# Tables' products at later steps of the routing, and gate products in quarters of TensorE's array

## The reference, cut to what matters

```python
scores = jnp.einsum('ntd,ed->nte', x, gate_w)            # 8 experts
probs = jax.nn.softmax(scores, axis=-1)
g, m = jax.lax.top_k(probs.transpose(0, 2, 1), k)        # k = 2 * 1024 / 8 = 256 tokens
xin = x[batch_idx, m]
h = gelu(jnp.einsum('nekd,edf->nekf', xin, w1))
h = jnp.einsum('nekf,efd->nekd', h, w2)
out = zeros.at[batch_idx, m].add(g[..., None] * h)
```

## Time and profile before

| | |
|---|---|
| median of 3 runs | 2249.83 us (2249.73 to 2259.84) |
| profiled execution | 2256.85 us, its span 2255.1 us |
| mean granted clock of PE over the span | 0.982 |
| PE busy | 2170.4 us, 96% |
| DVE, POOL, ACT busy | 1462.7, 1366.0, 1003.1 us |

### The profile page before, as it was taken

One profiled execution on the slowest core, in us unless ns is written; L12 is line 12 of the kernel. 1 busy time (PEld: TensorE's weight loads), 2 busy tenths in 40 slices (PEclk: granted clock), 3 DMA queues, 4 the chain that ended last, 5 costly groups with the idle time before them and its releaser, 6 DMA issues.

```text
span 2255.1 us, 34185 instructions
## 1 busy us (share of the span) xinstructions
PE 2170.4 (96%) x12186; PEld 1617.8 (72%) x12186; DVE 1462.7 (65%) x3348; ACT 1003.1 (44%) x1903; POOL 1366.0 (61%) x1237
## 2 busy tenths in 40 slices
PE   6998998999999999999999999999999999999997
PEld 4455888888886666666657766567666588899997
DVE  5355687676757666556775577874877645976653
ACT  3421443444445455335554354542554425444443
POOL 2322666677537766556775476664676845767774
PEclk9899999999999999999999999999999999999999
DMA  4332644555441122213212222212220244545552
GB/s 131 133 134 64 175 108 108 118 135 151 118 116 42 53 57 76 66 39 85 74 37 80 66 66 67 57 50 64 75 76 20 76 133 111 131 113 145 126 150 29
DMA packets 145049, 206.06 MB, mean 91 GB/s; under 512 B 19432, under 2 KB 112112, under 8 KB 144880
## 3 DMA queue, kind: packets, MB, share of 16 engines
q1 hardware_dynamic: 120304, 170.30, 25.4%
q0 software_dynamic: 24576, 33.57, 8.8%
HBM read 130.03 MB, written 39.85 MB: 75 GB/s over the span
## 4 chain that ended last, share of the span: by engine, by line
PE 75%; DVE 7%; POOL 3%; issue 3%; ACT 2%; DMA 1%; SPq 1%; another core or an unknown queue 0%; POOLq 0%; DVEq 0%; ACTq 0%
PE psum L1299 12%; PE psum L1278 12%; PE psum L1425 11%; PE psum L1327 7%; PE psum L1390 7%; PE psum L1406 6%; PE psum L1450 5%; PE psum L1341 4%; PE psum L1355 3%; PE psum L1435 3%; POOL t_acc L2362 2%; DVE f_hlo L2106 1%; PE psum L1368 1%; DVE f_hhi L2104 1%; PE psum L1246 1%
## 5 line engine op out<-in xcount | busy, mean ns | idle before, releaser
L1687 ACT ACTIVATE t_p<-psum 128x512 f32<-128x512 f32 (+3 forms) x768 | 323.6, 492 | 293.8 <-PE psum L1406 284.4
L2362 POOL TENSOR_TENSOR t_acc<-t_acc,t_p 128x1024 f32<-128x1024 f32 (+3 forms) x256 | 417.5, 1631 | 14.5 <-ACT t_p L1687 0.5
L2281 POOL TENSOR_TENSOR f_wlo<-f_wst,f_whi 128x256 fp32r<-128x256 f32 x256 | 219.9, 920 | 172.7 <-ACT f_whi L1620 172.7
L1299 PE MATMUL psum<-f_whi,f_hhi 128*128 128x256 f32 x1024 | 296.0, 289 | 6.2 <-DVE f_hlo L2106 6.2
L1425 PE MATMUL psum<-t_p,t_v 128*64 128x512 f32 (+3 forms) x1536 | 288.8, 496 | 6.2 <-POOL t_p L2342 6.2
L1299 PE MATMUL psum<-f_whi,f_hlo 128*128 128x256 f32 x1024 | 291.4, 285 | 0.0
L1299 PE MATMUL psum<-f_wlo,f_hhi 128*128 128x256 f32 x1024 | 291.1, 284 | 0.0
L2104 DVE CAST f_hhi<-f_h 128x512 fp32r<-128x512 f32 x256 | 135.0, 527 | 223.3 <-ACT f_h L1638 172.1
L1638 ACT ACTIVATE f_h<-psum 128x512 f32<-128x512 f32 x256 | 153.1, 599 | 280.9 <-PE psum L1278 235.9
L1390 PE MATMUL psum<-t_qa,t_ka 128*128 128x512 f32 (+3 forms) x768 | 223.1, 370 | 1.9 <-DVE t_kb L2136 0.7
L2362 POOL TENSOR_TENSOR t_acc<-t_p 128x768 f32<-128x768 f32 x64 | 134.5, 2102 | 135.4 <-PE psum L1435 132.1
(11 more groups left out here) (284 smaller groups left out, 4439.3 us busy)
## 6 DMA issues: line engine op xcount, KB each, us to landing
f_wst<-in_L_ffn_w SPq DMA_DIRECT2D x64, 1024.0 KB
t_ka<-t_ka SPq DMA_DIRECT2D x64, 256.0 KB, 3.5
t_qb<-t_qa SPq DMA_DIRECT2D x64, 256.0 KB, 3.7
t_wk<-wkT SPq DMA_DIRECT2D x32, 256.0 KB, 4.0
t_wq<-wqT SPq DMA_DIRECT2D x32, 256.0 KB, 4.0
t_wv<-wvT SPq DMA_DIRECT2D x16, 512.0 KB, 5.1
normal<-f_xy SPq DMA_DIRECT2D x5, 1024.0 KB, 10.2
a_x<-in_L_attn_a_x SPq DMA_DIRECT2D x4, 1024.0 KB, 10.1
```

Source lines behind the costliest of these rows:

```text
L1299: m = pe.matmul(out, h[:, js], w[:, f, :], start=(f == 0 and a == 0 and j % 2 == 0), stop=(f == FT - 1 and a == 2), skip_group_check=True)
L1687: act.activation(p[:, i, q0:], k.bank[bank][:, q0:], ACT.Exp, scale=1.0 / float(np.sqrt(k.DH))).then_inc(k.drained[bank], 1)
L2281: m = pool.tensor_tensor(t["wlo"][n % 2][:, i, ks], t["wst"][:, i, ks], t["whi"][n % 2][:, i, ks].bitcast(F32), ALU.subtract)
L2362: pool.tensor_tensor(acc[:, :, q0:], (p0 if kt == 1 else acc)[:, :, q0:], p[:, :, q0:], ALU.add).then_inc(k.p_acc, 1)
```

## The change

1. **Steps of the tables.** Thresholds get one step more before `threshold_rows` in routes 0, 1 and 3. The first sequence's table is no longer called behind its own column, but behind the second sequence's `hot_places` (in route 0 after four more empty steps). The second table comes after four (route 0) or two empty steps, together with the first `table_move`; the second `table_move` follows one (route 0) or three steps later. In route 0 the first table moves from step 39 to 44, the second from 43 to 49, of 56 steps.
2. **Gate products of routes 1 and 3.** `gateT` is widened with zeros to 32 columns per half of the channels. It is now the weights: 8 matmuls, each into 32 partitions of a bank (one quarter of the array's columns) with 256 tokens of `yT` passing. Scores then stand with experts on partitions. Two steps later `gate_turn` follows: ACT copies the bank's 128x256 into `wide`, and PE transposes it in two 128x128 blocks into the score bank, where `softmax_max` reads it with a stride of 32. So each sequence's scores take two more steps.
3. `pe_gate` goes; ACT's `row_transpose` waits for the bank of the gate product instead. A filling tile grows by 48 to keep addresses apart.

```diff
-        t["gate"], t["gateT"] = sb("f_gate", [E, D]), sb("f_gateT", [P, self.DT, E])
+        t["gate"], t["gateT"] = sb("f_gate", [E, D]), sb("f_gateT", [P, self.DT, 32])
...
+    def gated(self, t, i):
+        return t["wide"][:].rearrange("p n b e j -> p (n b e j)")[:, 2 * i * P:2 * (i + 1) * P]
...
         self.thresholds(r, t)
-        for _ in range(4 if r % 2 else 2):
+        for _ in range(5 if r % 2 else 3):
             yield
...
-        apart = [None] * 2 if r else []
+        steps = lambda first, later: [None] * (later if r else first)
         for i in range(2):
             self.hot_digits(r, i, t)
-            yield from apart
+            yield from steps(0, 2)
             self.hot_places(r, i, t)
-            yield
-            yield from apart
+            yield from steps(1, 2)
+            if i:
+                yield from steps(4, 0)
+                self.table(r, 0, t)
+                yield
             self.column(r, i, 0, t)
-            yield from apart
+            yield from steps(0, 2)
             self.column(r, i, 1, t)
-            yield
-            yield from apart
-            if i:
-                self.table_move(r, 0, pair[0], t)
-                yield
-            self.table(r, i, t)
-            yield
+            yield from steps(0, 2)
+        yield from steps(4, 2)
+        self.table_move(r, 0, pair[0], t)
+        self.table(r, 1, t)
+        yield from steps(1, 3)
         self.table_move(r, 1, pair[1], t)
         yield
...
             self.gate_product(r, i, t)
             yield
+            yield
+            self.gate_turn(r, i, t)
+            yield
...
     def gate_product(self, r, i, t):
...
-        for n in range(k.NBLK):
-            for dt in range(k.DT):
-                m = pe.matmul(sc[:, i, n, :], t["yT"][:, dt, n * P:(n + 1) * P], t["gateT"][:, dt, :],
-                              start=(dt == 0), stop=(dt == k.DT - 1))
-        m.then_inc(k.filled[b] if i else k.pe_gate, 1)
+        b = self.take(("gated", r, i), self.others[0])
+        for dt in range(k.DT):
+            rows = t["yT"][:, dt, :].rearrange("p (h g l) -> p h g l", h=2, l=P)
+            for g in range(4):
+                m = pe.matmul(k.bank[b][32 * g:32 * (g + 1), 0:2 * P], t["gateT"][:, dt, :], rows[:, :, g, :],
+                              start=(dt == 0), stop=(dt == k.DT - 1), skip_group_check=True)
+        m.then_inc(k.filled[b], 1)
...
+    def gate_turn(self, r, i, t):
+        k, pe = self.k, self.e
+        b, _ = k.where["score", r]
+        self.wait_drained(("gated", r, i))
+        for h in range(2):
+            m = pe.transpose(k.bank[b][:, (2 * i + h) * P:(2 * i + h + 1) * P], k.gated(t, i)[:, h * P:(h + 1) * P],
+                             k.ident[:])
+        if i:
+            m.then_inc(k.filled[b], 1)
...
+    def gate_turn(self, r, i, t):
+        k, act = self.k, self.e
+        b = self.wait_filled(("gated", r, i))
+        act.copy(k.gated(t, i), k.bank[b][:, 0:2 * P]).then_inc(k.drained[b], 1)
...
+        dve.memset(t["gateT"][:, :, k.E:], 0.0).then_inc(k.d_const, 1)
+        dve.tensor_copy(t["gateT"][:, :, 0:k.E], k.bank[b][:, 0:k.DT * k.E].rearrange(
             "p (k e) -> p k e", e=k.E)).then_inc(k.drained[b], 1)
...
+            row = 32 if r else k.E
+            sc = k.bank[b][:, 0:2 * k.NBLK * row].rearrange("p (n x) -> p n x", x=row)[:, :, 0:k.E]
```

More of the change, by code:

```diff
@@ L114, in semaphores @@
         self.d_scd = s("dve_early_scores")
-        self.pe_gate, self.a_probs = s("pe_gate"), s("act_probs")
+        self.a_probs = s("act_probs")
         self.a_split, self.d_split, self.p_split = s("act_whi"), s("dve_wlo"), s("pool_wlo")
@@ L271, in attention_tiles @@
         self.early_counts(st, early)
-        sb("t_room", [P, 64])
+        sb("t_room", [P, 112])
         heads(1)
@@ L412 @@
     mixed_norm = mixed_rows = mixed_transpose = mixed_gate = mixed_store = skip
-    route_load = route_store = row_transpose = gate_product = softmax_max = softmax_sum = prob_transpose = skip
+    route_load = route_store = row_transpose = gate_turn = gate_product = softmax_max = softmax_sum = prob_transpose = skip
     row_turn = row_scores = half_wide = count = digits = thresholds = threshold_rows = compare = rank = positions = skip
@@ L1147, in mixed_gate @@
             for dt in range(k.DT):
-                m = pe.matmul(sc[:, s, i, :], yT[:, s, dt, :], t["gateT"][:, dt, :], start=(dt == 0),
+                m = pe.matmul(sc[:, s, i, :], yT[:, s, dt, :], t["gateT"][:, dt, 0:k.E], start=(dt == 0),
                               stop=(dt == k.DT - 1), skip_group_check=True)
@@ L1170, in gate_product @@
         k, pe = self.k, self.e
-        b, _ = k.where["score", r]
-        sc = k.bank[b][:, 0:2 * k.NBLK * k.E].rearrange("p (b n e) -> p b n e", b=2, e=k.E)
         self.wait_drained(("gate", 0))
+        self.wait_ge(k.d_const, 8)
         for c in range(2):
@@ L1199, in row_scores @@
             for dt in range(k.DT):
-                m = pe.matmul(k.bank[bank][:, i * k.E:(i + 1) * k.E], t["yT"][:, i, dt, :], k.f[0]["gateT"][:, dt, :],
+                m = pe.matmul(k.bank[bank][:, i * k.E:(i + 1) * k.E], t["yT"][:, i, dt, :], k.f[0]["gateT"][:, dt, 0:k.E],
                               start=(dt == 0), stop=(dt == k.DT - 1))
@@ L1574, in row_transpose @@
         if i:
-            self.wait_ge(k.pe_gate, (r + 1) // 2)
+            self.wait_filled(("gated", r, 0))
         elif r == 1:
@@ L1788, in gate_transpose @@
         b = self.wait_filled(("gate", layer))
-        dve.tensor_copy(t["gateT"][:], k.bank[b][:, 0:k.DT * k.E].rearrange(
+        dve.memset(t["gateT"][:, :, k.E:], 0.0).then_inc(k.d_const, 1)
+        dve.tensor_copy(t["gateT"][:, :, 0:k.E], k.bank[b][:, 0:k.DT * k.E].rearrange(
             "p (k e) -> p k e", e=k.E)).then_inc(k.drained[b], 1)
@@ L1898, in softmax_max @@
             b = self.wait_filled(("score", r))
-            sc = k.bank[b][:, 0:2 * k.NBLK * k.E].rearrange("p (b n e) -> p (b n) e", b=2, e=k.E)
+            row = 32 if r else k.E
+            sc = k.bank[b][:, 0:2 * k.NBLK * row].rearrange("p (n x) -> p n x", x=row)[:, :, 0:k.E]
             taken = k.drained[b]
```

## The result

The changed kernel takes 2244.34 us (median of 9 runs, 2236.72 to 2245.88), the kernel before, now with nine runs as well, 2258.01 (2249.73 to 2263.76). The ratio is 0.9948, 95% interval 0.9930 to 0.9966: 8 to 16 us less, 11.7 at its middle. The forecast of 15.4 us is a ratio of 0.9932 and lies inside the interval, near its end; the forecast time of 2234.4 us is 9.9 us too low.

A forecast was written before the change was run, and what follows sets the result against it. PE (TensorE) bounds the kernel, busy 2170.4 of 2255.1 us. Terms 9.4 - 2.1 - 3.9 + 6.8 + 4.9 - 0.3 + 0.6 + 1.0 - 1.0 = 15.4 us off 2249.83 give 2234.4 us; range 2225 to 2247.

The forecast's parts named there:

- The time: Whole kernel: 15.4 us less than 2249.83, the median of the profiled execution's neighbours, giving 2234.4 us.
- Gate product: Four gate products, routes 1 and 3: quarters side by side take 1.05 us plus 0.1 for tiling changes; 9.4 us saved.
- Turns' transposes: After each gate product: two new PE transposes, taken as 4 records, 0.52 us each turn; 2.1 us lost in all.
- Turn waits: PE waits for ACT's gelu, then copy, at three of four turns, 1.3 us each; 3.9 us lost.
- a turn that waits over 2 us: At the gates' turns: listed as a sign that the prediction is wrong; waits of 1.3 us were expected.
- Clock: Behind the four gate products: none of the four half-clock falls remains, 1.7 us each; 6.8 us gained.
- Tables: Route 1's first table: its 3.30 us wait and the half clock behind it go, 4.9 us gained; route 3's tables 0.
- Ranks: Route 1's compare comes behind U3, so PE waits before rank: 1.3 us lost, net -0.3 with thresholds' 1.0 gain.
- Route 0's end: End of stage A: second table ends 1.9 us earlier, moving the gather, less half of 1.7; net 1.0 us gained.
- rival 5: More than forecast: the stall at 328 us dissolves too (3.7 us), ACT and DVE lose nothing; 2228 us, chance 0.05.
- Attention: The attention part between stage 0 and stage 1: forecast change 0 us.

The follow-up runs named there:

- a2: The changed kernel again, unchanged, on a second chip: 2240.86 us, 0.9941 of the kernel before.
- e3: Kernel before, with each gate product's 32 records cut into 12, 12 and 8 at three following steps: 2250.59 us, 1.0017 of the kernel before.
- e5: Changed kernel with 16 extra records of the quarters' shape, all into one quarter, ahead of each gate product: one run, 2260.52 us.
- a3: The changed kernel again, unchanged, on a third chip: 2244.30 us, 0.9949 of the kernel before.
- e2: Kernel before with only the gate products in quarters and their turns, all other steps as before: 2241.07 us, 0.9967 of the kernel before.
- e1: Kernel before with only the new steps of thresholds and tables, gate products as before: 2253.51 us, 1.0023 of the kernel before.
- e9: e1 with route 3's rank left at its old step: 2253.70 us, 0.9993 of the kernel before.

## Why the prediction was right and wrong

*The time: the step that failed.* 8.2 of the 9.9 us are the base, not the sum: I applied 15.4 us to 2249.83, a median of three, as it stood 0.3% below the profiled execution. With nine runs before's median is 2258.01. In the trace a step of this size shows near the program's start: PE stands at half clock there for 30.7 us in eight of the fourteen profiles and for 13.7 in four (17.1 and 27.3 in the other two), and the part up to route 0's rank is then 7.5 us shorter. These are windows of the kernel after and of a2, the same program:

```profile
45.00:76.00 31.00, 25.96 (x62) 10.73 (x61) 13.64 (x18) 21.91 (x32) 7.67 (x4) 0.51 0.00 1
```

```profile
45.00:76.00 31.00, 25.96 (x78) 11.38 (x79) 15.95 (x27) 23.05 (x35) 8.82 (x5) 0.78 0.03 9
```

Both kernels' runs fall into groups (2249.7 and 2256 to 2264; 2237 to 2239 and 2244 to 2246). Median against median, the change brought 13.7 us, by the ratio above 11.7; the sum of 15.4 is near the end of what was measured.

*Gate product*, forecast 9.4 us, right: sixteen records pass in 1.00 us before the next instruction, so 4 x (3.49 - 1.00) = 10.0. The changes of tiling cost nothing that shows; the next full-width record follows at 269.45. By the drain of which the Trainium skill speaks (TensorEngine Tiling (Array Packing), Key Properties) the product would have been longer than the estimate, not shorter; the trace doesn't bear it out.

*Turns' transposes*, -2.1: mis-sized. A transpose of 128x128 is one record, so a turn has two where it was worked out from four. PE's next instruction starts 0.14 to 0.27 us after the first of them, 0.8 us for the four turns.

*Turn waits*, 3 x 1.3: right in count and cause; in sum 4.6 instead of 3.9, by two errors that partly cancel. Two are 0.95: the copy takes 0.37 and not 0.475, it starts 0.49 after the gelu, and the signals take 0.04 and 0.05 and not 0.2 in all. The first is 2.74, for the delay above. The prediction had called a turn that waits over 2 us a sign of being wrong. The cause of this wait lies outside the kernel's order.

*Clock*, 6.8 us: right for this pair of profiles. None of the four falls is left. e3 and e5 show the mechanism from two sides. As 13 of 16 old products had a fall, an average execution had somewhat less to give. A fall can still come beside a long wait: a2, with 2.92 us before the turn, has one at 268.7; after and a3, with 2.74 and 2.94, have none.

*Tables*, 4.9 us: the step that failed in the sum. It took the 3.30 us before the table as a price that the tables' new steps save, whatever else changes. The gates' steps alone leave 0.73 of it (e2), and the tables' steps alone turn it into a wait for a low half at the same place (e1, e9) and gain nothing (e9, 0.9993). The table's column and the hidden rows come from the same DVE, which is the reason for both waits; moving the table changes which of its customers waits. Only with both halves' steps, in the kernel after, is neither this wait left nor a long one for a low half in its place. That the number came nearly out is owed to this interplay, which the sum didn't have, and is luck. In the table above stage 0 was to lose some 2 us of idle PE and has 0.7 us more; 1.4 us of this difference is the first turn's delay.

*Ranks*: route 1's new wait, forecast 1.3, is 1.34. Route 3's was not in the sum at all, and no reason was given: it is 1.42 where it was 0.64. Neither belongs to the thresholds' extra step. e2 and e3, which leave that step out and add two steps to each gate, wait 1.47 us each in route 1 and 2.70 and 2.68 in route 3; e1, which has only the step, waits for nothing in route 1 and 3.55 in route 3. Both together wait 1.34 and 1.42. These prices don't add either.

*Route 0's end*, 1.0: right in direction and reason (second table 2.3 us earlier, first `up` 1.7 us earlier, and a half-clock stretch of 10.2 us in one piece where there were two), 0.5 in size. The 1.97 us stall at 328 us with its fall did dissolve, as in rival 5, and paid for part of what was lost elsewhere; this was no part of the forecast's sum.

*Attention*, +1.7, is untouched by the change. Its half clock is 13.7 us in one profile of the kernel before and 23.9 in the other, 17.1, 23.9 and 17.1 in those of the kernel after; the term is one execution's.

## What to carry to other kernels

Before you credit a wait to a later step, list what else the releasing engine has in its queue at both places. When one engine serves several waits, measure each part of a change alone and all together, since their shares need not add: here one half cost 5 us alone and brought about 4 on top of the other. And take a base of many runs before a sum of 0.7% is put on it.

## What the hardware did that was not expected

- PE's clock: 16 matmuls of 8 columns in a row (3.5 us) brought 3.4 or 6.8 us at 1.2 GHz in 13 of 16 cases; the same in three pieces, or 256 columns in one quarter of the array for 3.4 us, in none of four each. Two waits of 1.74 us for a low half, 6 us behind unit 9's `xin` (e2 at 449.93, e3 at 454.11), brought none, one of 1.75 us at the same place in a3 (457.73) did: at this length a single profile decides nothing.
- DVE's four small compares at route 3 take 0.21 to 0.23 us each after (from 1962.80), but 0.54 and three times 0.76 in e1, where POOL works on a weight split from 1964.43 to 1967.47. In e9 POOL's split ends at 1966.97; the compare started at 1966.49 takes 0.56 us and the three from 1966.97 on 0.21 each. The kernel before shows the same: 0.56 for the one that starts before POOL's split ends at 1967.57, 0.21 for the three behind it. So 1.9 of e1's 3.55 us are DVE operations slowed beside POOL's.
- The delay behind the first gate, above, 0.8 to 2.6 us in ten of the fourteen profiles, has no record of its own on PE.
